# Four adjacency tiles on one DMA queue, the other early loads on the other

## What is computed

```
agg = einsum('ij,jh,ijh->ih', adj, x, T)        # layer 0; T = edge_table as (512, 512, 128)
gi = agg @ w_ih.T + b_ih
gh = x @ w_hh.T + b_hh
r, z = sigmoid(ir + hr), sigmoid(iz + hz)
x1 = layernorm(x + (1 - z) * tanh(in_ + r * hn) + z * x)
Wh = (x1 @ W) in 4 heads of 32                  # layer 1
e = leaky(s_src[i] + s_dst[j]), -9e15 where adj[i, j] is 0; attention = softmax(e over j)
out = layernorm(x1 + elu(attention @ Wh))
```

## Time and profile before

| | |
|---|---|
| median of 3 runs | 83.95 us |
| lowest and highest | 83.7 and 84.74 us |
| span of the profiled execution | 81.7 us, 1753 instructions |
| busy share | PE 79%, DVE 75%, POOL 65%, ACT 42% |
| DMA traffic | 2799 packets, 3.17 MB |
| mean granted TensorE clock | 0.888 of full speed |

### The profile page before, as it was taken

The page is one execution under the profiler, slowest core; times in us unless marked ns, Lnnn a source line. Parts: engine busy times, 40 slices in busy tenths (PEclk is TensorE's granted clock), DMA queues, the critical chain, the costliest instruction groups (busy, mean ns, idle before and its releaser), DMA issues.

```text
span 81.7 us, 1753 instructions
## 1 busy us (share of the span) xinstructions
PE 64.8 (79%) x612; PEld 47.4 (58%) x612; DVE 61.5 (75%) x197; ACT 34.0 (42%) x87; POOL 53.2 (65%) x74
## 2 busy tenths in 40 slices
PE   4996699999999997979984992089998797886300
PEld 4993354555998442279973741089786576664100
DVE  0099989562599996144997399999999999699760
ACT  0686990020200000006202303279979999974200
POOL 6848850478787879506925665596988965936450
PEclk9999995555599999999999999956999999999855
DMA  0999000012121210000000000000000000000111
GB/s 20 325 381 332 3 0 8 0 32 68 32 64 40 57 24 1 0 0 4 8 0 0 0 0 0 0 0 0 8 8 0 0 0 0 27 13 0 32 32 32
DMA packets 2799, 3.17 MB, mean 39 GB/s; under 512 B 451, under 2 KB 1990, under 8 KB 2790
## 3 DMA queue, kind: packets, MB, share of 16 engines
q1 hardware_dynamic: 1974, 1.71, 6.5%
q0 software_dynamic: 384, 0.63, 3.2%
q10 hardware_dynamic: 432, 0.72, 2.5%
HBM read 2.95 MB, written 0.26 MB: 39 GB/s over the span
## 4 chain that ended last, share of the span: by engine, by line
DVE 50%; PE 22%; issue 13%; POOL 5%; DMA 4%; ACT 1%; POOLq 1%; DVEq 1%
DVE tz L957 11%; DVE tz L978 7%; PE psG L545 6%; DMA adj_s<-adj_dram 4%; DVE onehot L841 4%; PE psG L546 4%; PE psD L635 3%; DVE key L761 3%; DVE rowv L765 3%; PE psG L642 2%; POOL rstd L375 2%; DVE mask L856 2%; DVE prT L986 2%; POOL tv L419 2%; DVE edge_p L891 2%
## 5 line engine op out<-in xcount | busy, mean ns | idle before, releaser
L419 POOL TENSOR_SCALAR tv<-tz,wh 128x512 f32<-128x512 f32 x16 | 15.1, 947 | 4.6 <-DVE mx L957 3.0
L358 POOL DMA_INDIRECT edge_t<-table_dram,idx_t x9 | 9.6, 1070 | 6.1 <-DVE idx_t L807 4.0
L978 DVE SCALAR_TENSOR_TENSOR tz<-tz,wh,tv 128x512 f32<-128x512 f32 x16 | 12.7, 803 | 0.8 <-POOL tv L419 0.7
L494 ACT ACTIVATE pr<-tz,nm 128x512 f32<-128x512 f32 x16 | 11.5, 717 | 2.9 <-DVE nm L971 2.4
L957 DVE CUSTOM_DVE_ANT_0 tz<-psG,mask 128x512 f32<-128x512 f32 x16 | 10.7, 681 | 1.7 <-PE psG L667 1.7
L540 PE MATMUL psA<-ones 128*128 128x128 f16 x142 | 10.3, 245 | 1.2 <-POOL ones L315 1.2
L540 PEld LDWEIGHTS psA<-ones 128*128 128x128 f16 x142 | 10.0, 111 | 1.2 <-POOL ones L315 1.2
L697 PE MATMUL psC<-ident,pr 128*128 128x128 f32 x32 | 5.7, 306 | 4.9 <-ACT pr L494 4.5
L635 PE MATMUL psD<-onehot,edge_p 128*128 128x512 f32 x18 | 8.2, 601 | 0.5 <-DVE edge_p L891 0.5
L375 POOL TENSOR_TENSOR rstd<-veps,mhalf 128x1 f32<-128x1 f32 (+1 forms) x6 | 3.7, 619 | 6.2 <-DVE veps L1029 4.7
L465 ACT ACTIVATE trz<-psG 128x512 f32<-128x512 f32 x2 | 1.2, 597 | 15.4 <-PE psG L643 15.4
(11 more groups left out here) (165 smaller groups left out, 141.6 us busy)
## 6 DMA issues: line engine op xcount, KB each, us to landing
adj_s<-adj_dram ACTq DMA_DIRECT2D x2, 256.0 KB, 3.9
adj_s<-adj_dram SPq DMA_DIRECT2D x2, 256.0 KB, 3.7
xT_s<-xT_dram SPq DMA_DIRECT2D x1, 256.0 KB, 4.3
x_s<-x_dram SPq DMA_DIRECT2D x1, 256.0 KB, 4.8
out_dram<-res SPq DMA_DIRECT2D x4, 64.0 KB, 1.6
whh_s<-w_hhT_dram ACTq DMA_DIRECT2D x1, 192.0 KB, 4.6
wih_s<-w_ihT_dram SPq DMA_DIRECT2D x1, 192.0 KB, 4.8
edge_t<-table_dram,idx_t POOLq DMA_INDIRECT x9, 2.6
```

The costliest lines, as they stand in the source:

```text
L358: pool.indirect_dma_start(buf[:, e, :], None, src, bass.IndirectOffsetOnAxis(ap=idx[:, e:e + 1], axis=0), bounds_check=src.shape[0] - 1, o ...
L419: pool.tensor_scalar(tv[:, q % A2, :], tz[:, q % A2, :], wh[:, t, H + h:H + h + 1], ALPHA, ALU.add, ALU.mult).then_inc(fifth_ready, 1)
L494: act.activation(pr[:, q % A2, :], tz[:, q % A2, :], ACT.Exp, bias=nm[:, t, h:h + 1], accum_out=den[:, t, h:h + 1]).then_inc(prob_ready, 1)
L978: dve.scalar_tensor_tensor(out=tz[:, q % A2, :], in0=tz[:, q % A2, :], scalar=wh[:, t, H + h:H + h + 1], in1=tv[:, q % A2, :], op0=ALU.add ...
```

## The change

The four adjacency tiles are issued one behind another on SP. The three bias pieces, `xT` and `x` go to ACT, where `w_hh` stands between `xT` and `x`. `w_ih`, `W` and `a` stay on SP, behind the four tiles. No semaphore, wait or computing instruction is changed.

```diff
@@ block.sync
-            sp.dma_start(adj_s[:, 0, :], adj_v[:, 0, :]).then_inc(adj_in[0], 16)
-            sp.dma_start(adj_s[:, 2, :], adj_v[:, 2, :]).then_inc(adj_in[2], 16)
-            sp.dma_start(brow[:, 0:3 * H], b_ih).then_inc(bias_in, 16)
-            sp.dma_start(brow[:, 3 * H:4 * H], b_hh[:, 2 * H:3 * H]).then_inc(bias_in, 16)
-            sp.dma_start(brz[:, :], b_hh[:, 0:2 * H]).then_inc(bias_in, 16)
-            sp.dma_start(xT_s[:, :], xT).then_inc(gru_in, 16)
-            sp.dma_start(x_s[:, :, :], x_v).then_inc(x_in, 16)
+            for t in range(NT):
+                sp.dma_start(adj_s[:, t, :], adj_v[:, t, :]).then_inc(adj_in[t], 16)
             sp.dma_start(wih_s[:, :], w_ihT).then_inc(wih_in, 16)
@@ block.scalar
-            act.dma_start(adj_s[:, 1, :], adj_v[:, 1, :]).then_inc(adj_in[1], 16)
-            act.dma_start(adj_s[:, 3, :], adj_v[:, 3, :]).then_inc(adj_in[3], 16)
+            act.dma_start(brow[:, 0:3 * H], b_ih).then_inc(bias_in, 16)
+            act.dma_start(brow[:, 3 * H:4 * H], b_hh[:, 2 * H:3 * H]).then_inc(bias_in, 16)
+            act.dma_start(brz[:, :], b_hh[:, 0:2 * H]).then_inc(bias_in, 16)
+            act.dma_start(xT_s[:, :], xT).then_inc(gru_in, 16)
             act.dma_start(whh_s[:, :], w_hhT).then_inc(gru_in, 16)
+            act.dma_start(x_s[:, :, :], x_v).then_inc(x_in, 16)
```

## The result

| | before | changed |
|---|---|---|
| median on one chip | 84.7 us (5 runs) | 85.68 us (5 runs, 85.37 to 87.09) |
| ratio to before | | 1.0255, 95% interval 1.0156 to 1.0355 |
| span of the profiled execution | 81.7 us | 84.8 us (execution 86.51 us) |

The account below looks back on a forecast made before the run. It took POOL's two jobs, started by ACT's first part of x, to hold `rowv` ahead of PE's matmuls. With L441 0.1 us earlier, 83.95 - 0.1 = 83.85, say 83.9 us; range 82.0 to 84.7.

Parts of the forecast that it names:

- What bounds the kernel now: DVE's `rowv` and first `reach` wait while POOL works; POOL's two jobs, not the last `max`, free `rowv`.
- 0.6 us short of being the bound: POOL's gather path: the third product was needed at 33.76 and ready at 33.14, so PE was the bound.
- rival 3: TensorE's clock stays at full speed after 12.2 for a few us more: 82.2 us; chance 0.05.
- The four tiles on SP: Adjacency loads: tile 0 lands 0.65 us earlier, near 3.5; `rowv` on DVE could start at 8.7, 0.4 us earlier.
- x, last on ACT: Load of x: L441 starts between 7.55 and 8.3, taken as 7.75, 0.1 us earlier than before.
- Biases, xT, w_hh: PE's part_of_h(0) can start 0.7 us earlier if w_hh is there by then; worth nothing on the path.
- Rival 4: PE idles longer before the matmuls on `rowv`, clock falls there, part_of_h(1) takes 3.6 us: 85.45 us; chance 0.08.
- Rivals 1 and 2: `rowv` runs before POOL's x work: 83.65 us, chance 0.14; with all eight `reach` ahead of L353 too: 82.15, chance 0.14.
- Rival 5: Tiles land no earlier or the last later; `rowv` ready 8.9 to 9.4, inside POOL's jobs: 83.9 us; chance 0.07.

Follow-up runs that it names:

- e8: Kernel before with POOL's two memsets (mhalf and edge_x) moved behind its last subtraction (L353); ratio 0.9981 to before.
- e1: Kernel before with only the adjacency moved: SP issues four tiles, then biases, xT, x, w_ih, W, a; ACT issues w_hh alone; 92.23 us, 1.002 of before.
- e15: Kernel before with 16 more matmuls on ones ahead of part_of_h(0) and 12 behind it; ratio 0.9995 to before.
- e5: Changed kernel without its three bias loads (POOL clears the bias row instead); ratio 1.0288 to before.
- e9: Changed kernel with the three biases on SP behind the four tiles; ACT issues xT, w_hh, x; ratio 1.0429 to before.
- e12: Changed kernel with biases and x on SP behind the four tiles; ACT issues only xT and w_hh; ratio 1.0259 to before.
- e11: Changed kernel itself, unaltered, measured again in the third batch; ratio 1.0413 to before.
- e6: Changed kernel with each bias load written as 16 pieces; 86.91 us.
- e16: Kernel before with 24 matmuls on ones in place of 62, every load where it was; ratio 1.0301 to before.
- e18: Kernel before with POOL's memsets ahead of the bias sum, more matmuls on ones, last four reach behind index(1); 83.74 to 93.13 us, no ratio.

## Why the prediction was wrong, step by step

**What bounds the kernel now**: right in the main. POOL's running instruction holds `rowv` and `reach` (e8, e1), though not the keys, and the gathers are right behind PE (e15). "0.6 us short of being the bound" was close enough to matter: rival 3 priced a clock that stays full at 82.2 us, and e15 had that clock up to 35.6 us and took the same time as before.

**The four tiles on SP**: tile 0 was right (first key 3.68, forecast near 3.6). The step that failed is the pair of late bounds: tile 2 by 5.9 and tile 3 by 7.1. They landed near 8.0 and 9.2, and tile 3 alone puts `rowv` at 11.23, where the forecast had it ready at 8.7. Both bounds came from one packet rate, about 400 GB/s from the earlier trace rows, taken as fixed whatever the order. It was half of that for two microseconds. And behind that, e5 and e9 show a second error, which needs no gap: three large loads on ACT have nothing ahead of them there, so they share the engines with tiles 2 and 3, and tile 3 lands near 8.0 at full rate.

**x, last on ACT**: L441 between 7.55 and 8.3; measured 11.02. The late bound was "the end of all early traffic", which is the right kind of bound, but it was put at 8.3 with the old rate.

**Biases, xT, w_hh**: the term was put at nothing ("It is worth nothing on the path"), and "0.7 earlier, if `w_hh` is there by then" carried a condition that was not priced. It was not there: it landed at 9.4, 7.1 us after issue, and `part_of_h(0)` started at 9.43 and not at 6.8. The chain starts at that load. A bound from both sides, by the same rule as for x, would have shown `part_of_h(0)` as the thing that can be late.

**The rivals.** Rival 4 had the size right (1.5 us; measured 1.55) and its test right (the clock did stand at 0.50 when the pair of tile 1 ran). Its cause was the reverse: PE's pause lay ahead of `part_of_h(0)`, because that was late, and not behind it. Rivals 1 and 2 had their condition, a short `rowv` in front of POOL's work, and got nothing from it, since `rowv` was ready at 11.07 only. Rival 5 had the direction (tiles land later because ACT's loads take their share) and stopped at 9.4 us for `rowv`, inside POOL's cover; it was 11.07.

The Trainium skill ("DMA: Bandwidth & Descriptors", Issuing engines are not separate DMA queues and Rules for kernel authors) says that the queues share 16 engines and that spreading loads over them saves issue time only. Of the tiles alone that holds here (e1, 1.002). Of the rest it does not: with all bytes the same, spreading the loads over the queues in another way moved `w_hh` from 4.6 to 7.1 us after issue and the total rate, from 4.5 to 5 us, from 393 to 164 GB/s.

**Still open**: what makes the gap; and what sets the time at which the clock falls. Filling the pauses put the fall off in each of three kernels (from 11.4 to 14.7 in the changed one, from 10.3 to 13.7 in e12, from 12.2 to 35.6 in the one before), so PE's pauses are shown to matter. Their length alone doesn't order the cases. The clock fell at 10.3 in e12, with two pauses of 0.59 and 0.21 us, but at 12.2 before, with 0.74 and 0.79, and at 13.0 in e5, with 2.05 us right ahead of the matmuls on `rowv`. And e11, the changed kernel again, had a pause of 1.33 us where the first profile had 2.99, and its clock fell at 10.0 in place of 11.4, inside `part_of_h(0)`. One thing that differs is when the clock first rose: at 6.9 and 6.6 us in e12 and e11, at 5.4 and 4.6 in the kernel before and the first profile of the changed one. No run varies this alone.

## To carry to other kernels

When loads change queues, give each its late bound from the order in which all queues compete, with a rate well below the one seen, and ask of each consumer, those off the path too, what happens if its load comes last. A condition in a sentence ("if it is there by then") is a term of the sum. Count PE's pauses ahead of the critical matmuls: here 55 more matmuls on ones filled one of 2.99 us and gave back the 1.55 us behind it, but look for the second bound before counting on it. And see in the trace that an edit did what it was meant to do: e6 left every packet as it was, and e16 took away more than it added.

## What was not expected of the hardware

- With three small bias loads ahead of large ones on ACT's queue and large ones on SP's, both queues ran at 164 to 236 GB/s for 2 us (before 393 to 406).
- TensorE at 1.2 GHz with a granted clock of 1.00 printed: the pair of L545 took 2.04 us in e16, whose first clock record is at 26.95 us, and 1.12 in the changed kernel, whose first is at 4.62.
- PE's clock fell at other times in two executions of the same kernel (11.4 and 10.0 us).
- The first gather starts 1.0 us behind its index, with or without DVE work in between (e18), the next ones 0.30 us behind one another.
